# Routing stage: prefix counts of the expert choices as nine TensorE products instead of GpSimd sums, and x of the first batch as second load of its queue

## The chip, the cores and the metric

The kernel runs on one core of one Trainium2 chip. The metric is the device time of one execution in microseconds. The trace of one profiled execution gives every instruction with its engine, its source line and what it waited for; its times are counted from the start of the span, which is the stretch from the first to the last instruction.

## The reference

Eight batches of 512 tokens with 256 features pass through a gated cross attention (each query keeps its 32 best keys of 1024) and a mixture of eight experts, each as a residual. What matters here is the routing between the two. Every token chooses its two best experts. For the first choices and the second choices apart, a token's place with its expert is the number of tokens before it, over all batches, that made the same choice. A token whose place is 640 or more is dropped.

```python
top_k_probs, top_k_idx = jax.lax.top_k(router_probs, TOP_K)     # TOP_K = 2
for k in range(TOP_K):
    eid = top_k_idx[:, k]
    onehot = (eid[:, None] == experts[None, :]).astype(jnp.int32)
    pos_all = jnp.cumsum(onehot, axis=0) - 1
    pos = jnp.take_along_axis(pos_all, eid[:, None].astype(jnp.int32), axis=1)[:, 0]
    valid = pos < capacity                                      # 640
    ...
    disp = jnp.zeros((E, capacity, D), x_flat.dtype).at[eid, pos_c].add(jnp.where(valid[:, None], x_flat, 0.0))
```

## The kernel before

The program has five stages, one after the other: `project` (queries, keys and values), `attend`, `repair` (the few attention tiles that have to be done again), `route` and `experts`. A stage begins on all engines when the one before it has ended. The change lies in `route` alone, which stands between about 2209 and 2368 us of the span.

`route` works batch by batch, eight of them, each with four tiles of 128 tokens. For a batch TensorE turns the attention output by eight transposes (L1187), ScalarE copies the result to SBUF (L1257), TensorE multiplies by the output weights (L1198), and VectorE adds the bias and the residual (L1297, L1298) and normalises (L1301 to L1327). For the batch before it TensorE turns the normalised rows (L1211) and forms the router's logits (L1220), and VectorE takes the best two experts (`choose`, L1312 to L1321). Nothing but the order in each engine's own program and the semaphores sets the order of the work.

SyncE issues all plain loads and stores of the stage from one queue. First come wo (the output weights, 256 KB), gate (8 KB), bo (128 KB) and the scalars g_xattn and g_ffn; these five count on one semaphore, `w_in`. TensorE, ScalarE and VectorE begin only when all five have landed. Then come x of batch 0 and of batch 1 (512 KB each, L1137), and later a store and a load for every further batch.

The places are counted in four groups of two batches, that is of eight tiles. When the choices of a group are known, VectorE writes them as one-hot rows (`mark`, L1351): for each of 128 tokens and each tile 16 numbers, two choices by eight experts. GpSimd forms `sofar`, the running sum of these rows over the tiles before, one addition for each tile (L1167). TensorE then makes two products into the same PSUM region, `places`: the triangular matrix `upto` by the group's one-hot rows counts the tokens up to this one within its tile (L1238), and the matrix of ones by the group's `sofar` counts all tiles before it (L1240). Both have 128 columns, 8 tiles by 16. VectorE picks the count that belongs to each choice (L1363, L1365) and makes of it the row number to send to (`slots`, up to L1378). GpSimd sends the group's normalised rows there by sixteen indirect DMAs (L1171), and only then turns to the sums of the next group.

In TensorE's program the products of a group come after the logits of the group's last batch and before the transposes of the next batch; for the last group they are the last work of the stage. `experts` reads the rows that were sent.

Of the kernel before, what the change touches and what calls it, by code (L numbers as in the profile page):

```python
# [10 lines left out]
ALU = mybir.AluOpType  # L11
# [3 lines left out]
P = 128  # L15
# [1021 lines left out]
def route(nc, pl, io, scr, out, keep):  # L1037
# [10 lines left out]
    C = K2 * E  # L1048
    attn, x1 = keep["attn"], keep["x1"]
    DX = pl.DX  # L1050
    with ExitStack() as ctx:
# [30 lines left out]
        onehot = sb("r_onehot", [P, TT, K2, E])  # L1082
        sofar = sb("r_sofar", [P, TT + 1, K2, E])
        place = sb("r_place", [P, GT, K2, E])
# [30 lines left out]
        hot = sem("r_hot")  # L1115
        added = sem("r_added")
        counted = sem("r_counted")
# [7 lines left out]
        @block.sync  # L1125
        def _(sp):
            sp.dma_start(wo[:], io["woT"].rearrange("(k p) n -> p k n", p=P)).then_inc(w_in, 16)
            sp.dma_start(gate[:], io["gateT"].rearrange("(k p) n -> p k n", p=P)).then_inc(w_in, 16)
            sp.dma_start(bo[:], io["bo"].partition_broadcast(P)).then_inc(w_in, 16)
            for i, name in enumerate(("g_xattn", "g_ffn")):  # L1130
                sp.dma_start(g[:, i:i + 1], io[name][0].partition_broadcast(P)).then_inc(w_in, 16)

            def load(b, u, start):
                if not start:
                    sp.wait_ge(x1_done, QT * (b - 1))
                    keep_x1(b - 2)
                sp.dma_start(xin[:, u], io["x"][b].rearrange("(t p) d -> p t d", p=P)).then_inc(x_in[u], 16)  # L1137

            def keep_x1(b):
                sp.dma_start(out[b].rearrange("(t p) d -> p t d", p=P), x1[:, bass.ds(b * QT, QT), :]).then_inc(x1_kept, 16)  # L1140

            over(sp, B, 2, load)
            for b in (B - 2, B - 1):
                sp.wait_ge(x1_done, QT * (b + 1))
                keep_x1(b)
            sp.wait_ge(x1_kept, 16 * B)

        @block.gpsimd
        def _(pool):
# [11 lines left out]

            nc.gpsimd.memset(sofar[:, 0], 0.0).then_inc(added, 1)
            for g in range(NG):
                pool.wait_ge(hot, g + 1)
                for t in range(g * GT, (g + 1) * GT):
                    pool.wait_ge(added, t + 1)
                    nc.gpsimd.tensor_tensor(sofar[:, t + 1], sofar[:, t], onehot[:, t], ALU.add).then_inc(added, 1)  # L1167
                pool.wait_ge(slots_done, g + 1)
# [8 lines left out]
        def _(pe):  # L1177
# [53 lines left out]
            def places(g):  # L1231

                pe.wait_ge(hot, g + 1)
                pe.wait_ge(added, g * GT + GT)
                if g:
                    pe.wait_ge(picked, g)
                tiles = slice(g * GT, (g + 1) * GT)
                nc.tensor.matmul(ps_n[:, 0:GT * C], upto[:], onehot[:, tiles].rearrange("p t k e -> p (t k e)"),  # L1238
                                 start=True, stop=False)
                nc.tensor.matmul(ps_n[:, 0:GT * C], ones[:], sofar[:, tiles].rearrange("p t k e -> p (t k e)"),  # L1240
                                 start=False, stop=True).then_inc(counted, 1)

# [42 lines left out]
        def _(dve):  # L1285
            count = [0]

            def link(ins):
                count[0] += 1
                ins.then_inc(own, 1)  # L1290
                dve.wait_ge(own, count[0])
# [63 lines left out]
            def slots(g):  # L1355
# [4 lines left out]
                link(V.tensor_scalar(first[:, n, 1], first[:, n, 1], float(CAP), None, ALU.add))  # L1360
                dve.wait_ge(hot, g + 1)
                dve.wait_ge(counted, g + 1)
                V.tensor_tensor(flat(place[:]), ps_n[:, 0:GT * C], flat(onehot[:, n]), ALU.mult).then_inc(picked, 1)  # L1363
# [390 lines left out]
```

## Time and profile before

| what | us |
|---|---|
| median of 3 runs | 3109.03 (3107.15 to 3109.63) |
| the profiled execution | 3109.36 |
| its span | 3107.6 |
| TensorE busy (matmuls) | 2532.3, 81% of the span |
| VectorE busy | 2635.3, 85% |
| ScalarE busy | 1733.3, 56% |
| GpSimd busy | 1676.1, 54% |

The span is shorter than the execution's own time by what lies around the first and the last instruction. A share of busy time is a mean over five stages with different limits, so it says little of one stage. A row of the timeline has the start, the duration, the engine, the line, the operation with its tiles, the number of instructions merged in it, and in brackets how long the engine had been idle before and what released it. The granted clock of TensorE stands as a share of its full 2.4 GHz.

### The profile page before, as it was taken

How to read it: one execution, taken by the hardware profiler on the slowest of the kernel's cores; microseconds unless marked ns; L12 is line 12 of the kernel's file. 1: busy time of each engine (PE TensorE's matmuls, PEld its weight loads, DVE VectorE, ACT ScalarE, POOL GpSimd, SP SyncE). 2: the span in 40 equal slices, each digit the busy share in tenths (PEclk: the TensorE clock that was granted, in tenths of full speed). 3: DMA queues.
4: the chain of work that ended last, by engine and by line, in shares of the span. 5: the costliest groups of instructions: out<-in, count | busy, mean ns of one | idle time of the engine just before them, and what ended most of it. 6: DMA issues, size and time to landing. Idle time of an engine off the chain costs nothing. (4 is left out here: it accounts for less than half of the span.)

```text
span 3107.6 us, 67900 instructions
## 1 busy us (share of the span) xinstructions
PE 2532.3 (81%) x18774; PEld 1650.4 (53%) x18775; DVE 2635.3 (85%) x19297; ACT 1733.3 (56%) x2250; POOL 1676.1 (54%) x2652
## 2 busy tenths in 40 slices
PE   7846888888888888888888888863472999999998
PEld 4522444444444444444444444432362999999998
DVE  5748999999999999999999999967563777777774
ACT  2215888887878888888888788851120222222222
POOL 1006777778787878787878787840062111111121
PEclk9977999999999999999999999995675999999999
DMA  6962121211211211212112112102233222222221
GB/s 184 264 186 67 39 68 30 53 53 31 68 39 30 68 39 40 59 39 56 42 39 68 30 43 63 30 1 56 71 131 115 66 65 55 71 55 58 67 45 17
DMA packets 132583, 202.25 MB, mean 65 GB/s; under 512 B 24112, under 2 KB 99120, under 8 KB 129136
## 3 DMA queue, kind: packets, MB, share of 16 engines
q1 hardware_dynamic: 108048, 167.65, 20.0%
q0 software_dynamic: 17920, 29.52, 4.5%
q8 instruction: 149, 2.44, 0.3%
q14 instruction: 226, 1.85, 0.2%
q10 hardware_dynamic: 6240, 0.79, 0.2%
HBM read 130.48 MB, written 69.50 MB: 64 GB/s over the span
## 5 line engine op out<-in xcount | busy, mean ns | idle before, releaser
L596 DVE MAX8 a_cand<-a_sc 128x8 f32<-128x43 f32 (+1 forms) x12288 | 1602.6, 194 | 48.4 <-ACT a_sc L535 48.3
L702 POOL TENSOR_SCALAR a_side<-a_sc,a_top 128x1024 bf16<-128x1024 f32 x256 | 729.2, 2848 | 0.0
L535 ACT COPY a_sc<-a_ps_s 128x1024 f32<-128x1024 f32 x512 | 516.7, 1009 | 162.9 <-PE a_ps_s L437 155.9
L546 ACT ACTIVATE a_pT<-a_ps_e 128x1024 f32<-128x1024 f32 x512 | 521.8, 1019 | 86.1 <-PE a_ps_e L458 71.3
L454 PE MATMUL a_ps_e<-a_floor,a_onesb 128*128 128x256 bf16 x1024 | 283.8, 277 | 284.8 <-issue 145.8
L1461 POOL DMA_INDIRECT out<-e_y,e_xin x80 | 124.1, 1552 | 608.9 <-ACT e_y L1586 564.3
L722 POOL TENSOR_SCALAR a_gone<-a_cand,a_top 128x80 f32<-128x80 f32 x512 | 293.8, 574 | 261.0 <-DVE a_top L630 260.7
L456 PE MATMUL a_ps_e<-a_big,a_side 128*128 128x128 bf16 x4096 | 398.9, 220 | 0.0
L458 PE MATMUL a_ps_e<-a_qs,a_ks 99*128 99x512 bf16 x1024 | 395.0, 386 | 0.0
L528 ACT ACTIVATE a_side<-a_sc,a_next_under 128x1024 bf16<-128x1024 f32 x256 | 295.1, 1153 | 169.7 <-POOL a_next_under L715 169.7
L490 PE MATMUL a_ps_o<-a_pT,a_vs 128*32 128x512 f32 x2048 | 369.5, 603 | 1.1 <-ACT a_pT L546 1.1
L437 PE MATMUL a_ps_s<-a_ks,a_qs 96*128 96x512 bf16 x1024 | 319.1, 394 | 57.7 <-DMA a_vs<-scr_v 50.9
L1518 PE MATMUL e_ps_gu<-e_xh,e_wl 128*128 128x256 f32 x1280 | 361.9, 283 | 5.0 <-DVE e_xl L1597 5.0
L456 PEld LDWEIGHTS a_ps_e<-a_big,a_side 128*128 128x128 bf16 x4096 | 316.6, 98 | 92.2 <-issue 1.1
L1519 PE MATMUL e_ps_gu<-e_xl,e_wh 128*128 128x256 f32 x1280 | 361.5, 282 | 0.0
L1520 PE MATMUL e_ps_gu<-e_xh,e_wh 128*128 128x256 f32 x1280 | 361.3, 282 | 0.0
L454 PEld LDWEIGHTS a_ps_e<-a_floor,a_onesb 128*128 128x128 bf16 x1024 | 100.4, 98 | 490.5 <-ACT a_pT L546 260.5
L468 PE MATMUL a_ps_c<-a_side,a_row_of 128*16 128x512 bf16 x1024 | 314.0, 389 | 4.2 <-POOL a_side L702 2.8
L1578 ACT ACTIVATE e_th<-e_ps_gu 128x256 f32<-128x256 f32 x320 | 123.4, 386 | 323.0 <-PE e_ps_gu L1520 323.0
L1638 DVE SCALAR_TENSOR_TENSOR e_sg<-e_th,e_ps_gu 128x256 f32<-128x256 f32 x320 | 135.0, 422 | 184.0 <-ACT e_th L1578 168.9
L1518 PEld LDWEIGHTS e_ps_gu<-e_xh,e_wl 128*128 128x128 f32 x1280 | 242.3, 189 | 5.8 <-DVE e_xl L1597 5.8
L1519 PEld LDWEIGHTS e_ps_gu<-e_xl,e_wh 128*128 128x128 f32 x1280 | 242.4, 189 | 0.0
(211 smaller groups left out, 4908.0 us busy)
## 6 DMA issues: line engine op xcount, KB each, us to landing
scr_v<-p_vp SPq DMA_DIRECT2D x32, 512.0 KB, 5.9
a_vs<-scr_v SPq DMA_DIRECT2D x32, 512.0 KB, 5.9
a_mask<-in_mask SPq DMA_DIRECT2D x32, 512.0 KB, 6.8
scr_k<-p_kp SPq DMA_DIRECT2D x96, 128.0 KB, 2.4
a_ks<-scr_k SPq DMA_DIRECT2D x32, 384.0 KB, 4.7
a_qs<-scr_q SPq DMA_DIRECT2D x192, 64.0 KB, 5.2
scr_disp<-a_blank SPq DMA_DIRECT2D x16, 650.0 KB, 8.3
e_xin<-scr_disp SPq DMA_DIRECT2D x40, 260.0 KB, 2.7
```

What stands on the lines that cost most here:

```text
L437: mm = nc.tensor.matmul(ps_s[:, h * 512:(h + 1) * 512], qs[0:KR, u, j, qt * P:(qt + 1) * P], ks[0:KR, u, j, h * 512:(h + 1) * 512], start= ...
L454: nc.tensor.matmul(ps_e[:, i * S + HALF * P:(i + 1) * S], onesb[:], floor[:], start=True, stop=False)
L456: nc.tensor.matmul(ps_e[:, i * S + qt * P:i * S + (qt + 1) * P], side[:, (QT * H + qt) % SIDES, keys], big[:], start=False, stop=False)
L458: mm = nc.tensor.matmul(ps_e[:, i * S:(i + 1) * S], ks[:, u, j, keys], qs[:, u, j, :], start=False, stop=True)
L490: mm = nc.tensor.matmul(ps_o[VW * c:VW * (c + 1), :], vs[:, u, k, VW * j:VW * (j + 1)], pT[:, k, :], start=(half == 0), stop=(half == 1), ...
L535: nc.scalar.copy(sc[:, T % SCORES, :], ps_s[:]).then_inc(copied, 1)
L546: nc.scalar.activation(pT[:, 2 * n:2 * n + 2, :].rearrange("p k q -> p (k q)"), ps_e[:], ACT.Exp).then_inc(expd, 1)
L596: ins = nc.vector.max(c[:, 8 + n:8 + n + 7 * CH + 1:CH], sc[:, T % SCORES, pl.cut[n]:pl.cut[n + 1]])
L702: nc.gpsimd.tensor_scalar(side[:, T % SIDES, :], sc[:, T % SCORES, :], top[:, T // TILES % 2, T % TILES, pl.TOPK - 1:pl.TOPK], None, ALU.is_lt
L1518: nc.tensor.matmul(out, al, bh, start=(k == 0), stop=False)
L1519: nc.tensor.matmul(out, ah, bl, start=False, stop=False)
L1520: mm = nc.tensor.matmul(out, ah, bh, start=False, stop=(k == n - 1))
```

## The change

Two things are changed in `route`.

The running sums leave GpSimd. TensorE forms them with shifted products: the triangular matrix by the eight tiles of the group as before, then seven products of the matrix of ones by the first 7, 6, ... 1 tiles of the group, each added to the PSUM region 1, 2, ... 7 tiles further right, and a last product of ones by `sofar` of the group, the counts of all groups before it, read once for each of the eight tiles. `sofar` has now one entry for each group. VectorE keeps it: in `slots` it sums the group's one-hot rows over the tiles and adds the result to the group's entry. GpSimd only sends rows.

On SyncE's queue x of batch 0 comes directly behind wo, and bo comes before gate.

```diff
             sp.dma_start(wo[:], io["woT"].rearrange("(k p) n -> p k n", p=P)).then_inc(w_in, 16)
+            sp.dma_start(xin[:, 0], io["x"][0].rearrange("(t p) d -> p t d", p=P)).then_inc(x_in[0], 16)
+            sp.dma_start(bo[:], io["bo"].partition_broadcast(P)).then_inc(w_in, 16)
             sp.dma_start(gate[:], io["gateT"].rearrange("(k p) n -> p k n", p=P)).then_inc(w_in, 16)
-            sp.dma_start(bo[:], io["bo"].partition_broadcast(P)).then_inc(w_in, 16)
             ...
-                sp.dma_start(xin[:, u], io["x"][b].rearrange("(t p) d -> p t d", p=P)).then_inc(x_in[u], 16)
+                if b:
+                    sp.dma_start(xin[:, u], io["x"][b].rearrange("(t p) d -> p t d", p=P)).then_inc(x_in[u], 16)
             ...
-            nc.gpsimd.memset(sofar[:, 0], 0.0).then_inc(added, 1)
+            nc.gpsimd.memset(sofar[:, 0], 0.0).then_inc(summed, 1)
             for g in range(NG):
-                pool.wait_ge(hot, g + 1)
-                for t in range(g * GT, (g + 1) * GT):
-                    pool.wait_ge(added, t + 1)
-                    nc.gpsimd.tensor_tensor(sofar[:, t + 1], sofar[:, t], onehot[:, t], ALU.add).then_inc(added, 1)
                 pool.wait_ge(slots_done, g + 1)
             ...
                 pe.wait_ge(hot, g + 1)
-                pe.wait_ge(added, g * GT + GT)
+                pe.wait_ge(summed, g + 1)
                 if g:
                     pe.wait_ge(picked, g)
-                tiles = slice(g * GT, (g + 1) * GT)
-                nc.tensor.matmul(ps_n[:, 0:GT * C], upto[:], onehot[:, tiles].rearrange("p t k e -> p (t k e)"),
-                                 start=True, stop=False)
-                nc.tensor.matmul(ps_n[:, 0:GT * C], ones[:], sofar[:, tiles].rearrange("p t k e -> p (t k e)"),
-                                 start=False, stop=True).then_inc(counted, 1)
+                t0 = g * GT
+                wide = lambda n: onehot[:, t0:t0 + n].rearrange("p t k e -> p (t k e)")
+                nc.tensor.matmul(ps_n[:, 0:GT * C], upto[:], wide(GT), start=True, stop=False)
+                for d in range(1, GT):
+                    nc.tensor.matmul(ps_n[:, d * C:GT * C], ones[:], wide(GT - d), start=False, stop=False)
+                nc.tensor.matmul(ps_n[:, 0:GT * C].rearrange("p (t c) -> p t c", c=C), ones[:],
+                                 sofar[:, g].unsqueeze(1).broadcast_to([P, GT, C]), start=False, stop=True
+                                 ).then_inc(counted, 1)
             ...
                 dve.wait_ge(hot, g + 1)
+                if g + 1 < NG:
+                    link(V.tensor_reduce(here[:, g], onehot[:, n].rearrange("p t k e -> p (k e) t"), AX_X, ALU.add))
+                    dve.wait_ge(summed, g + 1)
+                    V.tensor_tensor(sofar[:, g + 1], sofar[:, g], here[:, g], ALU.add).then_inc(summed, 1)
                 dve.wait_ge(counted, g + 1)
```

## Rows read from the trace of the kernel before

**Rows 1.** The page: the chain that ended last, shares by line.

```profile
PE e_ps_gu L1518 5%; PE e_ps_gu L1519 5%; PE e_ps_gu L1520 5%; PE e_ps_y L1520 2%; PE e_ps_y L1518 2%; PE e_ps_y L1519 2%; PE e_ps_x L1510 1%; DVE e_wl L1621 0%; DMA e_raw<-in_wdT 0%; DMA e_raw<-in_wgT 0%; POOL out L1461 0%; DMA out<-e_y,e_xin 0%; DVE e_hl L1606 0%; DVE e_wh L1614 0%; DVE e_hh L1602 0%
```

**Rows 2.** Timeline of the stage's begin: start, duration, engine, line, idle before.

```profile
2211.63 0.43 SPq L1131 DMA_DIRECT2D r_g<-in_g_ffn  x1
2212.11 1.24 SPq L1137 DMA_DIRECT2D r_xin<-in_x  x2
...
2216.06 1.97 PE L1187 MATMUL r_ps_a<-r_ident,attn 128*128 128x128 f32 x8 [8.22 <-DMA r_g<-in_g_ffn]
...
2221.27 0.42 DVE L1297 TENSOR_TENSOR r_aO<-r_ps_w,r_bo 128x256 f32<-128x256 f32 x1 [12.08 <-PE r_ps_w L1198]
```

**Rows 3.** DMA issues of 2209 to 2212.2 us: count, KB, us to landing.

```profile
r_xin<-in_x SPq DMA_DIRECT2D x1, 512.0 KB, 5.5
...
r_g<-in_g_ffn SPq DMA_DIRECT2D x1, 0.5 KB, 4.4
```

**Rows 4.** Windows: length, busy by engine (count), PE clock, DMA share, GB/s.

```profile
2216.50:2217.00 0.50, 0.50 (x5) 0.50 (x4) 0.00 (x0) 0.00 (x0) 0.00 (x0) 0.50 1.09 385
```

**Rows 5.** Timeline around the first inner group.

```profile
2249.75 0.36 DVE L1351 TENSOR_TENSOR r_onehot<-r_lane,r_chosen 128x64 f32<-128x64 f32 x2
...
2250.20 2.41 POOL L1167 TENSOR_TENSOR r_sofar<-r_sofar,r_onehot 128x16 f32<-128x16 f32 x8 [39.10 <-DVE r_onehot L1351]
...
2252.46 0.77 PE L1238 MATMUL r_ps_n<-r_onehot,r_upto 128*128 128x128 f32 x2 [5.92 <-POOL r_sofar L1167]
...
2253.45 1.91 PE L1187 MATMUL r_ps_a<-r_ident,attn 128*128 128x128 f32 x8
2253.79 0.29 DVE L1363 TENSOR_TENSOR r_place<-r_ps_n,r_onehot 128x128 f32<-128x128 f32 x1 [1.85 <-PE r_ps_n L1240]
...
2258.68 0.42 DVE L1297 TENSOR_TENSOR r_aO<-r_ps_w,r_bo 128x256 f32<-128x256 f32 x1 [2.16 <-PE r_ps_w L1198]
```

**Rows 6.** Windows around the first inner group, columns as in rows 4.

```profile
2254.00:2256.00 2.00, 2.00 (x9) 1.69 (x8) 1.69 (x10) 1.17 (x2) 0.00 (x0) 0.50 0.00 0
...
2258.00:2260.00 2.00, 2.00 (x11) 1.77 (x10) 1.25 (x3) 0.00 (x0) 1.59 (x2) 0.99 0.19 67
```

**Rows 7.** Timeline of the second and third group: one-hot rows, next residual.

```profile
2278.35 0.36 DVE L1351 TENSOR_TENSOR r_onehot<-r_lane,r_chosen 128x64 f32<-128x64 f32 x2
...
2286.61 0.42 DVE L1297 TENSOR_TENSOR r_aO<-r_ps_w,r_bo 128x256 f32<-128x256 f32 x1 [1.54 <-PE r_ps_w L1198]
...
2306.08 0.36 DVE L1351 TENSOR_TENSOR r_onehot<-r_lane,r_chosen 128x64 f32<-128x64 f32 x2
...
2314.13 0.42 DVE L1297 TENSOR_TENSOR r_aO<-r_ps_w,r_bo 128x256 f32<-128x256 f32 x1 [1.34 <-PE r_ps_w L1198]
```

**Rows 8.** Weight loads of passes with 8 columns; loads and products of L437.

```profile
2316.92 1.86 PEld L1220 LDWEIGHTS r_ps_l<-r_gate,r_xT 128*128 128x128 f32 x16 [0.54 <-issue]
...
2325.30 3.49 PEld L1220 LDWEIGHTS r_ps_l<-r_gate,r_xT 128*128 128x128 f32 x16 [0.29 <-issue]
...
L437 PEld LDWEIGHTS a_ps_s<-a_ks,a_qs x1024: 95/98/181, 245.5 to 2048.4; 96*128 96x128 bf16 x171
L437 PE MATMUL a_ps_s<-a_ks,a_qs x1024: 377/382/634, 245.5 to 2048.6; 96*128 96x512 bf16 x171
```

**Rows 9.** Timeline of the last group and the stage's end.

```profile
2330.82 0.36 DVE L1351 TENSOR_TENSOR r_onehot<-r_lane,r_chosen 128x64 f32<-128x64 f32 x2
...
2333.82 2.33 POOL L1167 TENSOR_TENSOR r_sofar<-r_sofar,r_onehot 128x16 f32<-128x16 f32 x8
...
2337.29 0.29 DVE L1363 TENSOR_TENSOR r_place<-r_ps_n,r_onehot 128x128 f32<-128x128 f32 x1 [5.82 <-PE r_ps_n L1240]
...
2340.80 0.99 POOL L1171 DMA_INDIRECT scr_disp<-r_xn,r_slot_to  x1 [4.64 <-DVE r_slot_to L1378]
...
2359.99 0.97 POOL L1171 DMA_INDIRECT scr_disp<-r_xn,r_slot_to  x1 [0.31 <-issue]
2368.21 0.38 SPq L1477 DMA_DIRECT2D e_raw<-in_wgT  x1
```

More of the change, by code:

```diff
@@ L1082, in route @@
         onehot = sb("r_onehot", [P, TT, K2, E])
-        sofar = sb("r_sofar", [P, TT + 1, K2, E])
+        here = sb("r_here", [P, NG, C])
+        sofar = sb("r_sofar", [P, NG, C])
         place = sb("r_place", [P, GT, K2, E])
@@ L1115, in route @@
         hot = sem("r_hot")
-        added = sem("r_added")
+        summed = sem("r_summed")
         counted = sem("r_counted")
```

## The prediction

> **What bounds the kernel now.** I first read the chain of work that ended last: it is nearly all TensorE in the expert stage, and no line of the routing stage stands in it [rows 1]. That chain starts over at every stage boundary: the expert stage's first transfer is issued at 2368.21, after the last row of the routing stage has been sent [rows 9]. So the routing stage, 2209 to 2368 us of the span, has an end of its own, and what is taken out of its own chain moves everything behind it as a block. I then read that stage as a timeline. The reader is to see three things. It begins with a wait for small loads [rows 2]. In the middle VectorE and TensorE hand over to each other, with GpSimd between them once for each group of two batches [rows 5]. It ends with sixteen sends by GpSimd that nothing covers [rows 9].
>
> **The loads (x of the first batch second).** Before, the scalar g_ffn is issued at 2211.63, and its landing, 4.4 us later, starts TensorE at 2216.06 [rows 2, 3]. TensorE, ScalarE and VectorE all wait for the same count of five loads, wo, gate, bo and the two scalars. x was issued at 2212.11 and landed 5.5 us later, at 2217.6 [rows 2, 3]. VectorE needs it first at 2221.27, and what it waited for there was TensorE's product [rows 2]. Landing x earlier is therefore worth nothing: it was 3.7 us early already. Its cost is that gate, bo and the scalars are issued one issue later on SyncE's queue. Two x issues took 1.24 us, so 0.62 us each [rows 2]. If g_ffn keeps its 4.4 us, TensorE starts 0.6 us later. The bounds are these. Below: g_ffn now lands as its twin g_xattn might, which was issued one place before it and had no x directly behind it; I give that -0.4 us at most, an estimate, since g_ffn's 4.4 us is the only row for it. Above: the whole of x passes first, 512 KB at the 385 GB/s that the queue moved while x came in [rows 4], 1.4 us. I take +0.6 us, and it counts in full, because every engine of the stage hangs on that start.
> The Trainium skill, page DMA: Bandwidth & Descriptors, section Queues, rings and completion order, says that on each DMA engine descriptors are consumed in ring order. This speaks against the move, as bytes of x put ahead of the scalars are then waited for: by that rule the price is nearer the upper bound than the 0.6.
>
> **The three inner groups (after batches 1, 3 and 5).** In the first of them the one-hot rows are done at 2249.75 + 0.36 = 2250.11. GpSimd takes them up 0.09 us later and adds tile by tile for 2.41 us. TensorE starts its two products at 2252.46, goes on to the transposes of the next batch at 2253.45 (so 0.99 us for two products), and VectorE takes the counts 0.34 us later, at 2253.79 [rows 5]. The change takes GpSimd's sums out and puts seven products in: nine instead of two. A product of this type is two passes, as x2 on the row of one product shows [rows 5]. A pass with 128 x 128 weights costs its weight load even when only 8 columns stream: sixteen such passes took 3.49 us in the last batch, 0.218 each, and 1.86 us, 0.116 each, one batch before [rows 8]. That is the clock at 1.2 and at 2.4 GHz. Nor does the shared matrix of ones save its loads: where two products share weights in the attention stage, there are 1024 loads for 1024 products [rows 8]. Around the first group the granted clock was 0.50, that is 1.2 GHz [rows 6]. So 14 more passes cost 14 x 0.218 = 3.05 us there. TensorE can start at 2250.11 + 0.09 = 2250.20, ends at 2250.20 + 0.99 + 3.05 = 2254.24, and the transposes behind it in its queue start 0.79 us later than before. VectorE's counts are as late. By this alone the next batch's residual, which waited 2.16 us for TensorE [rows 5], is 0.79 us later in each group.
> Against that stands the clock. It was back at 2.4 GHz from 2258 on [rows 6], 5.5 us after the products had begun at 2252.46 [rows 5]. The products now begin 2.26 us earlier. If the rise comes as long after their start, it falls at 2250.11 + 5.6. The eight passes of the transposes end at 4.13 + 8 x 0.218 = 5.9 us after the one-hots, and the eight passes of the first half of the output product behind them run at 2.4 GHz: 256 columns each, at most 2 x 0.116, so 1.9 us in all (an estimate). VectorE would start the residual at about 7.8 us after the one-hots. Before it was 8.57 us (2258.68 - 2250.11), and 7.90 and 7.69 us in the second and third group [rows 5, 7]. That gives -0.8, -0.1 and +0.1. The bounds for a group are +0.79 (no earlier rise) and, with everything at 2.4 GHz, the wait of the residual as it stood, -2.16, -1.54 and -1.34 [rows 5, 7]. The three together give -0.8 and lie between -5.0 and +2.4; as the bounds reach further down than up, I take -1.0 us.
> VectorE's two new instructions (a sum over tiles and one addition) read no more than the 128 x 128 that the row of the count takes 0.29 us for, so 0.6 us at most, and lie in the 1.85 us that it waited for TensorE [rows 5]. Were that wait gone, they would cost 0.6 us a group. The running count that they write is needed by TensorE one group later, 28 us on. GpSimd's own work shrinks, and its sends start when the slots are done, as before.
>
> **The last group.** Here GpSimd's sums were late. The one-hots are done at 2330.82 + 0.36 = 2331.18, but GpSimd is still sending the third group's rows and starts adding at 2333.82. VectorE gets the counts at 2337.29, the first send is at 2340.80, the last at 2359.99, and the next stage at 2368.21 [rows 9]. After the change TensorE needs only the one-hots and an old count: 2331.18 + 0.09 + 0.99 + 3.05 + 0.34 = 2335.65, so 1.64 us earlier. GpSimd ended the old sends before 2333.82, so it is not late for the new ones. The sixteen sends stay as they are and move as a block. At 2.4 GHz the 18 passes would take 18 x 0.116 = 2.1 us, and the gain would be some 3.6 us. TensorE had been at 1.2 GHz shortly before [rows 8], so I take -2.0, nearer to that end.
> The Trainium skill, page TensorE: Matmul & The Clock Gate, section Back-to-back issue gap, gives the isolated spacing of products by the columns streamed. The seven products stream 448 columns where seven full ones would stream 896, so by that rule the added passes cost half, 1.5 us instead of 3.05. The row of the 8-column passes speaks against it [rows 8], and the page itself adds that weight loads share in the spacing.
>
> **Sum.** +0.6 - 1.0 - 2.0 = -2.4 us. The profiled execution took 3109.36 us, of which the span is 3107.6; it would take 3107.0. The median of the runs shown, 3109.03, lies 0.3 lower, so I forecast 3106.6 us.
>
> **The rivals.**
> (a) TensorE becomes the bound in the inner groups: the nine products run at 1.2 GHz, the rise comes when it came, and each of the three groups is 0.79 us later. 2.4 + 0.6 - 1.64 = +1.4 us, 3110.4, slower than before. It decides as soon as the three delays and the later start exceed the last group's gain. For it: clock 0.50 around the products [rows 6]. Against it: the earlier start of TensorE's work.
> (b) A narrow product costs its columns: four groups at 1.5 us less, of which the inner three can use only their waits. About -2.4 - 4 = -6.4 us, or 3102.6. The 8-column row is against it [rows 8]. It is the rule of the Trainium skill's page TensorE: Matmul & The Clock Gate named above.
> (c) x holds the scalars back for its whole transfer: +1.4 in place of +0.6, 3107.4. The order of the queue is for it; the share of idle time in the queue before x is not shown at that place.
> (d) The clock is at 2.4 GHz in all four groups: up to -5.0 - 3.6 + 0.6 = -8 us, 3101.0.
> (e) It does not matter: GpSimd's sends bind the last group anyway. The 3.5 us between the counts and the first send, with GpSimd idle [rows 9], speak against this; 3109.
>
> **How the numbers follow.** Forecast 0.58, (a) 0.13, (b) 0.05, (c) 0.14, (d) 0.04, (e) 0.06. The forecast's own range is some 2.5 us to either side, from the unknown rise of the clock and the run to run spread of 2.5 us that the three times show. Leaving out (b), (d) and part of (a), the range is 3103.0 to 3110.0. 0.2% is 6.2 us, about what a measurement can tell from no change: faster needs 3102.8 or less, which takes (d), half of (b) and a tail of the forecast, 0.07; slower needs 3115.2, which no case reaches, 0.01; within it 0.92.
>
> **What would show it.** TensorE's first product of the stage should start 0.4 us early to 1.4 us late, by when g_ffn lands. Each group should show 18 passes that start 0.1 us after the one-hots, at 0.22 us each. The wait of VectorE for the counts should be longer in the inner groups and shorter, by about 1.6 us, in the last; the first send of the last group should come 4.5 + 3.5 = 8.0 us after the one-hots instead of 9.6. The forecast is wrong if passes of few columns cost less than 0.2 us at 1.2 GHz, if the stretch from the stage's start to the last one-hots moves by more than 3 us, or if the expert stage behind it changes its length.

## The result

The changed kernel takes 3114.7 us (median; 3111.6 to 3118.3), the kernel before 3109.9 us beside it. The ratio is 1.0015, 95% interval 1.0009 to 1.0021: slower by 4.8 us, 2.8 to 6.5 by the interval. The forecast was 3106.6 us, 3103.0 to 3110.0. The profiled execution took 3114.59 us with a span of 3112.3; against 3109.36 before it is 5.2 us longer.

Between the two traces these 5.2 us lie as follows. The stages before `route` ended 0.9 us earlier, `route` took 1.3 us more (159.8 against 158.5, from the issue of wo to the issue of the first expert weights), `experts` 4.3 us more (743.7 against 739.4), and 0.5 us lies around the span. So most of the loss stands in a stage that the change does not touch.

**The loads after.** The rows are the issue of the last scalar, its size and us to landing from the view of DMA issues, and TensorE's first work:

```profile
2211.25 0.43 SPq L1133 DMA_DIRECT2D r_g<-in_g_ffn  x1
...
r_g<-in_g_ffn SPq DMA_DIRECT2D x1, 0.5 KB, 4.0
...
2215.32 0.90 PE L1186 MATMUL r_ps_a<-r_ident,attn 128*128 128x128 f32 x3 [8.41 <-DMA r_g<-in_g_ffn]
```

wo is issued at 2208.75, so TensorE starts 6.57 us after it; before it was 6.38 (2209.68 to 2216.06).

**The first group after** (rows of the timeline: start, duration, engine, line, operation, in brackets the wait and its releaser). The lines are moved by the change: L1354 is the one-hot rows, L1239 to L1242 the nine products, L1186 and L1197 the next transposes and output product, L1300 the residual.

```profile
2249.13 0.36 DVE L1354 TENSOR_TENSOR r_onehot<-r_lane,r_chosen 128x64 f32<-128x64 f32 x2
2249.55 0.80 PE L1239 MATMUL r_ps_n<-r_onehot,r_upto 128*128 128x128 f32 x2 [3.49 <-DVE r_onehot L1354]
2250.14 3.01 PE L1241 MATMUL r_ps_n<-r_onehot,r_ones 128*128 128x112 f32 x14
2252.98 0.77 PE L1242 MATMUL r_ps_n<-r_sofar,r_ones 128*128 128x128 f32 x2
2253.55 1.92 PE L1186 MATMUL r_ps_a<-r_ident,attn 128*128 128x128 f32 x8
2253.80 0.29 DVE L1370 TENSOR_TENSOR r_place<-r_ps_n,r_onehot 128x128 f32<-128x128 f32 x1 [1.90 <-PE r_ps_n L1242]
...
2258.58 0.42 DVE L1300 TENSOR_TENSOR r_aO<-r_ps_w,r_bo 128x256 f32<-128x256 f32 x1 [2.06 <-PE r_ps_w L1197]
```

The products start 0.06 us after the one-hot rows' end, the seven new ones take 3.01 us, which is 0.215 us a pass, and the counts come 4.67 us after the one-hots' start instead of 4.04 [rows 5]. All that was foreseen. What was not is the clock. The windows of TensorE over the first and the third group after (columns: stretch, length, busy time of TensorE's products PE, its weight loads PEld, VectorE DVE, ScalarE ACT and GpSimd POOL with counts, granted clock, busy share of the DMA engines, GB/s):

```profile
2252.00:2254.00 2.00, 2.00 (x11) 2.00 (x11) 0.20 (x1) 0.00 (x0) 0.00 (x0) 0.50 0.00 0
...
2256.00:2258.00 2.00, 2.00 (x7) 1.61 (x6) 0.49 (x4) 0.09 (x1) 0.27 (x1) 0.56 0.06 16
2258.00:2260.00 2.00, 2.00 (x11) 1.73 (x10) 1.33 (x3) 0.00 (x0) 1.70 (x2) 1.00 0.19 67
...
2312.00:2314.00 2.00, 2.00 (x6) 1.64 (x6) 1.10 (x7) 0.58 (x1) 0.00 (x0) 0.50 0.00 0
2314.00:2316.00 2.00, 2.00 (x7) 1.61 (x6) 0.11 (x1) 0.00 (x0) 1.68 (x2) 0.56 0.18 67
```

In a window that begins at 0.50, ends at 1.00 and has a mean of 0.56, the clock rose 0.24 us before the end, here at 2257.76 and 2315.76. The products of these groups had begun at 2249.55 and 2306.27, so the clock came 8.2 and 9.5 us after them. In the kernel before it came 5.6 us after them in the first group; in the third the window of before gives 2312.64, 3.9 us after the start at 2308.74:

```profile
2312.00:2314.00 2.00, 2.00 (x9) 1.71 (x8) 0.72 (x5) 0.26 (x1) 0.43 (x1) 0.84 0.00 0
```

**The last group and the stage's end after:**

```profile
2332.58 0.36 DVE L1354 TENSOR_TENSOR r_onehot<-r_lane,r_chosen 128x64 f32<-128x64 f32 x2
...
2337.35 0.29 DVE L1370 TENSOR_TENSOR r_place<-r_ps_n,r_onehot 128x128 f32<-128x128 f32 x1 [4.11 <-PE r_ps_n L1242]
...
2340.86 0.97 POOL L1170 DMA_INDIRECT scr_disp<-r_xn,r_slot_to  x1 [6.56 <-DVE r_slot_to L1385]
...
2360.01 0.97 POOL L1170 DMA_INDIRECT scr_disp<-r_xn,r_slot_to  x1 [0.30 <-issue]
...
2368.57 0.38 SPq L1484 DMA_DIRECT2D e_raw<-in_wgT  x1
```

The counts come 4.77 us after the one-hots' start, before 6.47 [rows 9], a gain of 1.70 us. But the one-hots themselves come later: 83.45 us after those of the first group, where it was 81.07 [rows 5, 9].

**The expert stage.** Two places differ. The first is its first weight load: the DMA issues of the first 7 us, after and then before (KB, us to landing), with the instruction queue's line where there is one:

```profile
q14 instruction: 1, 0.01, 0.3%
...
e_raw<-in_wgT SPq DMA_DIRECT2D x1, 1024.0 KB, 5.7
```
```profile
e_raw<-in_wgT SPq DMA_DIRECT2D x1, 1024.0 KB, 4.9
```

VectorE waits for this load and TensorE's first transposes wait for VectorE. They start 19.0 us into the stage instead of 17.7. The second place is the one at which VectorE's loop over experts (`Fori`, experts 3 and 4, then 5 and 6) jumps back, some 460 us into the stage. VectorE's first row behind the jump, before and after:

```profile
2826.87 0.69 DVE L1597 TENSOR_TENSOR e_xl<-e_ps_x,e_xh 128x512 fp32r<-128x512 f32 x1 [2.83 <-issue]
```
```profile
2830.22 0.69 DVE L1604 TENSOR_TENSOR e_xl<-e_ps_x,e_xh 128x512 fp32r<-128x512 f32 x1 [3.73 <-issue]
```

"issue" says that VectorE waited for nothing that the profile shows. In the 4.5 us ahead of these rows the DMA view has one instruction packet on queue q14 before and two after:

```profile
q14 instruction: 1, 0.01, 0.5%
```
```profile
q14 instruction: 2, 0.02, 1.4%
```

Behind this pause TensorE's clock fell in the changed kernel, from 1.00 to 0.66 in the mean of five microseconds, with 29 products instead of some 44:

```profile
2831.00:2836.00 5.00, 5.00 (x29) 5.00 (x30) 0.85 (x2) 0.76 (x2) 2.89 (x2) 0.66 0.46 52
2836.00:2841.00 5.00, 5.00 (x44) 5.00 (x43) 4.56 (x15) 1.16 (x4) 0.00 (x0) 1.00 0.22 53
```

### The profile page after: what moved, and what is told of

Read it like the earlier page. It is cut to its first block and busy times, and to the rows that moved or that the text cites. A ratio compares the mean times of both kernels' runs of the same rounds, so it can differ in the third digit from the quotient of the medians.

```text
span 3112.3 us, 67985 instructions
## 1 busy us (share of the span) xinstructions
PE 2544.3 (82%) x18830; PEld 1664.3 (53%) x18831; DVE 2637.1 (85%) x19303; ACT 1731.8 (56%) x2250; POOL 1668.0 (54%) x2620
## 5 line engine op out<-in xcount | busy, mean ns | idle before, releaser
L596 DVE MAX8 a_cand<-a_sc 128x8 f32<-128x43 f32 (+1 forms) x12288 | 1637.5, 206 | 48.2 <-ACT a_sc L535 48.2
L437 PE MATMUL a_ps_s<-a_ks,a_qs 96*128 96x512 bf16 x1024 | 318.3, 393 | 57.5 <-DMA a_vs<-scr_v 50.8
```

The lines of the kernel that those rows point to most:

```text
L437: mm = nc.tensor.matmul(ps_s[:, h * 512:(h + 1) * 512], qs[0:KR, u, j, qt * P:(qt + 1) * P], ks[0:KR, u, j, h * 512:(h + 1) * 512], start= ...
L596: ins = nc.vector.max(c[:, 8 + n:8 + n + 7 * CH + 1:CH], sc[:, T % SCORES, pl.cut[n]:pl.cut[n + 1]])
```

## The experiments

The table has what the runs' traces and times say, each stretch from one trace. "Intervals" are from the one-hots of one group to those of the next. "Counts" is from the last group's one-hots' start to VectorE's first use of the counts. "Landing" and "pause" are the two places of the expert stage named above. A median with an interval of the ratio was timed beside the kernel before; one without is a single time.

| kernel | intervals, sum | counts | `route` | landing | pause | `experts` | time, ratio |
|---|---|---|---|---|---|---|---|
| before | 28.6 + 27.7 + 24.7 = 81.1 | 6.5 | 158.5 | 4.9 | 2.83 | 739.4 | 3109.9 |
| changed | 28.9 + 27.8 + 26.7 = 83.5 | 4.8 | 159.8 | 5.7 | 3.73 | 743.7 | 3114.7, 1.0015 [1.0009, 1.0021] |
| e1 before again | 25.1 + 31.4 + 24.9 = 81.4 | 6.5 | 159.5 | 5.0 | 2.83 | 739.7 | 3111.3 |
| e2 loads only | 28.5 + 27.5 + 24.9 = 80.9 | 6.5 | 158.1 | 4.8 | 2.97 | 739.5 | 3109.6, 0.9999 [0.9990, 1.0008] |
| e3 counts only | 29.0 + 27.8 + 26.7 = 83.6 | 4.8 | 160.4 | 5.6 | 3.82 | 744.1 | 3114.7, 1.0015 [1.0006, 1.0024] |
| e4 VectorE's part only | 27.4 + 28.8 + 24.9 = 81.0 | 6.5 | 158.8 | 5.6 | 3.89 | 741.0 | 3112.5, 1.0008 [0.9999, 1.0017] |
| e5 last group only | 27.4 + 28.9 + 24.9 = 81.2 | 4.8 | 157.9 | 5.1 | 2.90 | 740.4 | 3108.3, 0.9995 [0.9986, 1.0004] |
| e6 changed, 119 more | 29.0 + 27.8 + 26.8 = 83.5 | 4.8 | 160.1 | 5.0 | 2.88 | 739.4 | 3111.1, 1.0003 [0.9994, 1.0012] |
| e7 before, 128 more | 28.6 + 27.5 + 24.9 = 81.0 | 6.5 | 158.8 | 4.9 | 2.88 | 739.6 | 3111.1 |
| e9 full width (e8, a single run) | 26.6 + 25.4 + 24.6 = 76.7 (76.3) | 4.3 (4.3) | 152.2 (151.4) | 5.6 (5.5) | 3.94 (3.73) | 741.1 (740.7) | 3104.6, 0.9984 [0.9975, 0.9993] (3102.4) |
| e10 full width, 119 more | 26.6 + 25.4 + 24.7 = 76.7 | 4.3 | 152.6 | 5.0 | 2.84 | 739.5 | 3101.7, 0.9976 [0.9967, 0.9985] |
| e11 before, extra products | 26.4 + 29.8 + 24.2 = 80.4 | 7.3 | 158.1 | 4.9 | 2.95 | 739.7 | 3109.3, 1.0001 [0.9991, 1.0010] |
| e12 before, 40 more | 27.4 + 28.9 + 25.2 = 81.5 | 6.0 | 158.9 | 5.0 | 2.88 | 739.6 | 3110.3 |

**Which part loses.** Three runs take the change apart, beside one of the kernel before as it is. e2 has only the new order of the loads, e3 only the counts.

> The kernel before, unchanged: a second look at its stages. Every theory expects the median of before within its spread of some 3 us. What is asked is how far the three places vary by themselves that were longer in the changed kernel: the first weight load of the expert stage (4.9 us before, 5.7 after), the pause of VectorE in the middle of that stage (2.8 us before, 3.7 after) and TensorE's clock behind it. If they are a matter of VectorE's program, they come out as before: 2.8 us and no fall of the clock. If they are chance, they may come out either way.

> Only the loads are reordered, the counts are formed as before. Theory loads (the 512 KB of x hold the scalars back): +0.6 to +1.4 us. Theory program (VectorE's longer program costs the time, in the expert stage): no change, within 0.5 us, as VectorE's program is the one of before. Theory counts: no change.

> Only the counts move to TensorE, the loads stay in the old order. Theory loads: -2 to -3 us, since the loss would be in the order of the loads. Theory program: +4 to +5 us, as in the whole change, with a VectorE pause of 3.7 us in the expert stage. Theory counts (the nine products delay the inner groups): +1 to +2 us, all of it inside the routing stage.

e2 stands at 0.9999 and e3 at 1.0015: the loads cost nothing that can be measured, and the counts are the whole loss. In both e2 and the changed kernel the stage's first work after the loads starts 6.5 to 6.6 us after the issue of wo; the eight kernels with the old order (before, e1, e3, e4, e5, e7, e11, e12) have 5.8 to 6.8, so no difference shows there either.

**VectorE's part alone.** The kernel before, with the same number of VectorE instructions added at the same place as in the change, their results unused; TensorE and GpSimd do what they did.

```diff
+                if g + 1 < NG:
+                    link(V.tensor_reduce(spare[:, g], onehot[:, n].rearrange("p t k e -> p (k e) t"), AX_X, ALU.add))
+                    dve.wait_ge(own, count[0])
+                    V.tensor_tensor(spare_sum[:, g], spare[:, g], spare[:, g], ALU.add).then_inc(spared, 1)
                 dve.wait_ge(counted, g + 1)
```

> The kernel before with VectorE's six new instructions alone (three sums over tiles and three additions, into tiles that nothing reads), so that VectorE's program is as long as in the changed kernel; GpSimd forms the sums and TensorE makes two products, as before. Theory program: +3 to +4.5 us, the pause of VectorE in the middle of the expert stage 3.7 instead of 2.8 us and the clock of TensorE down to 1.2 GHz behind it. Theory counts and theory loads: no change, within 0.5 us, as the six instructions lie in VectorE's wait for the counts.

`route` is as before (158.8), so the instructions themselves cost nothing there. But the landing and the pause are those of the changed kernel, and `experts` is 741.0 instead of 739.4. The fall of the clock behind the pause, which the text expected, did not come. The time, 1.0008 with an interval from 0.9999 to 1.0017, agrees with those 1.6 us but would not show them by itself. So these two places follow VectorE's program, not TensorE's or GpSimd's. Is it the length, or where the code of the loop comes to lie? With the waits among them the change adds nine instructions to VectorE's program.

```diff
             slots(NG - 1)
+            for i in range(119):
+                V.memset(spare[:, i:i + 1], 0.0)
```

e6 puts these 119 into the changed kernel, e7 puts 128 and e12 puts 40 into the kernel before. VectorE has nothing to do there until the next stage; the 119 took 2.89 us of that time.

> The changed kernel, with 119 very small VectorE instructions (a memset of one column each) behind its last work of the routing stage, where VectorE waits some 25 us for the last sends. With the change's nine added VectorE instructions these make 128. In the trace an instruction packet of VectorE's size is 8192 bytes; I take it as 128 instructions. Theory A (what counts is where the code of the expert stage lies in such blocks): VectorE's pause in the middle of the expert stage is 2.8 us again instead of 3.7, the first weights land 4.9 us after their issue instead of 5.7, TensorE's first transposes start 17.5 to 18 us into the stage, and TensorE's clock no longer falls behind the pause; the expert stage takes 739.5 to 741 us and the time is 3 to 4 us below the changed kernel, so 1 to 2 us above the kernel before, which is what the routing stage lost. Rival B (what counts is the length of VectorE's program): pause 3.7 to 3.9 us, expert stage 743.7 or more, time as the changed kernel's. Rival C (the expert stage is longer for TensorE's 28 added rows or for GpSimd's shorter program): as B, but with the pause at 2.8.

> The kernel before with 128 of the same small VectorE instructions at the same place. Theory A (place in blocks): everything in the expert stage as in the kernel before: pause 2.8 us, first weights 4.9 us. Rival B (length): pause 3.7 us or more, first weights 5.6 us, expert stage 741 us.

> The kernel before with 40 of the small VectorE instructions behind its last work of the routing stage, for a second place of the expert stage's code in its blocks. Nine more gave a pause of 3.7 to 3.9 us and first weights after 5.6 to 5.7 us, 128 more 2.88 and 4.9. Theory A (it matters whether a block's border falls in front of the loop's start): pause again of one of the two sizes, 2.8 to 3.0 or 3.7 to 3.9, and the first weights 4.9 to 5.1 or 5.6 to 5.7 independently of it. Rival B (the pause grows with the place): something between or beyond, such as 4.5 us.

With 119 more the pause is short again:

```profile
2829.54 0.69 DVE L1607 TENSOR_TENSOR e_xl<-e_ps_x,e_xh 128x512 fp32r<-128x512 f32 x1 [2.88 <-issue]
```
```profile
q8 instruction: 1, 0.02, 1.4%
q14 instruction: 1, 0.01, 0.6%
```

One packet on q14 instead of two (the one on q8 did not lengthen the pause), the first weights after 5.0 us, `experts` 739.4, no fall of the clock, and the ratio 1.0003 instead of 1.0015, although VectorE's program is longer still. That is theory A: it is the place that counts, not the length. What is left, +2.1 us by the medians and +1.0 by the ratio (interval -1.9 to +3.7), agrees with the 1.6 us that `route` is longer. Of the places tried, 0, 40 and 128 instructions further give the short pause and the early landing; 9 gives the long ones, in each of the five kernels that had it (changed, e3, e4, e8, e9). In the changed kernel and e3 the clock fell behind the long pause, in e4, e8 and e9 it did not. What decides that was not tried. With the fall `experts` took 743.7 and 744.1, without it 740.7 to 741.1, so some 2.9 us go with it. (Both kernels also have an earlier fall, 39 us into the stage. e1, e2, e5 and e12 have one too, at 37 to 39 us, and take 739.5 to 740.4, so it explains little of this.)

**The last group alone.** GpSimd sums the inner groups as before; TensorE forms the counts of the last group with the nine products.

```diff
-                pe.wait_ge(added, g * GT + GT)
+                pe.wait_ge(added, g * GT + (GT if g + 1 < NG else 1))
...
+                if g + 1 < NG:
+                    nc.tensor.matmul(ps_n[:, 0:GT * C], ones[:], sofar[:, tiles].rearrange("p t k e -> p (t k e)"),
+                                     start=False, stop=True).then_inc(counted, 1)
+                    return
...
+                for d in range(1, GT):
+                    nc.tensor.matmul(ps_n[:, d * C:GT * C], ones[:], wide(GT - d), start=False, stop=False)
...
```

> The kernel before, with one thing of the change: only in the last group do TensorE's nine products form the counts; the three inner groups stay with GpSimd's sums, the loads stay in the old order, VectorE's program is unchanged. Theory A (the loss has two places: the inner groups, where TensorE's products take 0.65 us more each and the clock rises no earlier, and the expert stage, where VectorE's nine added instructions move its code): here neither is touched, so the last group's counts come 1.5 to 1.7 us earlier, the stretch from the stage's start to the choices of the last group stays at 121 us, the routing stage is 156.5 to 157 us long instead of 158.5, the expert stage stays at 739.4 to 739.8, and the time is 1.5 to 2 us below the kernel before. Rival B (any change of the routing stage's length costs the expert stage some us by its phase): the routing stage gets shorter and the expert stage is 741 to 744 all the same. Rival C (the products of the last group are of no use because GpSimd's old sends hold it): routing stage 158.5, time as before.

The last group's counts come 4.76 us after its one-hots, 1.7 us earlier, as expected, and VectorE's program, landing and pause are as before or nearly (5.1, 2.90). `route` was 157.9, 0.6 us shorter and not 1.5 to 2; `experts` was 740.4. What hides the gain lies ahead of the change: from the issue of wo to the first group's one-hots e5 took 41.0 us, the kernel before 40.1, and over all runs this stretch goes from 39.7 to 41.0. The time is 0.8 us lower in the median, and the interval reaches from -4.4 to +1.2 us: the gain of the last group is there in the trace but is not shown in the time.

**The width of the passes.** The changed kernel, but all seven products stream 128 columns. Each group's one-hot rows stand behind eight tiles of zeros, and the product for a shift of d tiles reads from d tiles further back.

```diff
-        onehot = sb("r_onehot", [P, TT, K2, E])
+        onehot = sb("r_onehot", [P, NG, 2 * GT, K2, E])
...
+            nc.gpsimd.memset(onehot[:, :, 0:GT], 0.0).then_inc(made, 1)
...
-                    nc.tensor.matmul(ps_n[:, d * C:GT * C], ones[:], wide(GT - d), start=False, stop=False)
+                    nc.tensor.matmul(ps_n[:, 0:GT * C], ones[:], back(d), start=False, stop=False)
```

> The changed kernel, but every one of the seven products streams the full 128 columns: the one-hot rows of each group stand behind eight tiles of zeros, and the product for a shift of d tiles reads from d tiles further back. Same count of passes, of waits and of VectorE instructions. Theory A (the pass costs its weight load, and TensorE's clock rises late in the changed kernel because narrow passes keep the engine less busy): a pass costs 0.22 to 0.25 us at 1.2 GHz as the narrow ones did (0.215 to 0.218), and the clock rises some 5 us after the products' start, as before, instead of 6.5 to 9.5 us; the choices of the last group come 1 to 3 us earlier than in the changed kernel (117.1 us after TensorE's start of the stage). Rival B (the rise does not depend on the width): rises 6.5 to 9.5 us after the products' start, choices at 117 us or later.

> The changed kernel with the seven products at full width, as in the run of one look (3102.4 us), now timed. There the routing stage was 151.3 us long (158.5 before, 159.9 changed) and the granted clock rose 4.3, 5.3 and 3.2 us after the products' start (8.2, 6.5 and 9.5 changed). Theory A (the width of the passes, through the clock, decides): median 3102 to 3106, the routing stage 151 to 155 us, the expert stage 740.8 to 741.5 as VectorE's code still lies nine instructions further. Rival B (the one look was a chance of the clock's timing): median 3109 to 3113, routing stage 157 us or more.

(In the third group of e8, the rise came 3.8 us after the products' start, not the 3.2 that the second of these texts says.) Timed, the kernel takes 3104.6 us, 0.9984 of the kernel before, and `route` 152.2 us. This is theory A: the pass costs the same and the clock comes earlier. Its size was not foreseen: the three intervals are 7 us shorter than in the changed kernel, where the first text has 1 to 3. Nor do the rows show its reason, a less busy engine: over the passes TensorE is busy 2.00 of 2.00 us with either width (2252 to 2254 above, 2254 to 2256 in e10). e10 has in addition the 119 instructions.

> Both repairs: the seven products at full width, and 119 small VectorE instructions behind its last work of the routing stage, so that its code for the expert stage lies 128 instructions further instead of nine. Theory A (two independent causes): routing stage 151 to 155 us, pause 2.8 to 2.9, first weights 5.0 us, expert stage 739.4 to 740; median 1 to 2 us below the full-width kernel without them, 3101 to 3104.5, and 5 to 8 us below the kernel before. Rival B (the effects are not additive): as the full-width kernel.

e10 takes 3101.7 us, ratio 0.9976 (0.9967 to 0.9985): some 7.5 us faster than the kernel before and the best version of the study. In the traces the two repairs add up (`route` 152.6, `experts` 739.5); by the times alone the intervals of e9 and e10 overlap. Its first and third group (the lines moved by one or two more):

```profile
2252.57 0.80 PE L1240 MATMUL r_ps_n<-r_onehot,r_upto 128*128 128x128 f32 x2 [3.48 <-DVE r_onehot L1355]
2253.16 3.19 PE L1242 MATMUL r_ps_n<-r_onehot,r_ones 128*128 128x128 f32 x14
...
2260.36 0.42 DVE L1301 TENSOR_TENSOR r_aO<-r_ps_w,r_bo 128x256 f32<-128x256 f32 x1 [0.83 <-PE r_ps_w L1199]
...
2304.63 0.80 PE L1240 MATMUL r_ps_n<-r_onehot,r_upto 128*128 128x128 f32 x2 [3.96 <-DVE r_onehot L1355]
...
2312.01 0.42 DVE L1301 TENSOR_TENSOR r_aO<-r_ps_w,r_bo 128x256 f32<-128x256 f32 x1 [0.45 <-PE r_ps_w L1199]
```
```profile
2257.00:2259.00 2.00, 1.76 (x10) 1.47 (x10) 1.70 (x9) 1.07 (x2) 0.00 (x0) 0.90 0.00 0
...
2308.00:2310.00 2.00, 1.76 (x13) 1.52 (x12) 1.03 (x5) 0.73 (x2) 0.00 (x0) 0.85 0.08 27
```

The fourteen passes stream 1792 columns and not 896. Their row is 0.18 us longer than the narrow ones', by the last pass, but their weight loads take 3.11 us in both kernels (changed first, then e10), and the counts come 4.66 us after the one-hots' start (changed kernel 4.67):

```profile
2249.93 3.11 PEld L1241 LDWEIGHTS r_ps_n<-r_onehot,r_ones 128*128 128x128 f32 x14
```
```profile
2252.95 3.11 PEld L1242 LDWEIGHTS r_ps_n<-r_onehot,r_ones 128*128 128x128 f32 x14
```

The means of 0.90 and 0.85 put the rise at 2257.4 and 2308.6, 4.8 and 4.0 us after the products' start. In the changed kernel it was 8.2 and 9.5. VectorE's residual waits 0.83 us, where it waited 2.06 in the changed kernel.

Is the earlier rise only a matter of when the clock had fallen? In the first group that is excluded. The windows ahead of it, of the changed kernel and of e10, begin at 1.00 and end at 0.50, so their means put the fall at 2247.5 and 2250.6, in both kernels 2.0 us before the products' start:

```profile
2247.00:2249.00 2.00, 0.00 (x0) 0.00 (x0) 1.83 (x20) 1.49 (x2) 0.00 (x0) 0.63 0.55 184
```
```profile
2250.00:2252.00 2.00, 0.00 (x0) 0.00 (x0) 1.83 (x21) 1.49 (x2) 0.00 (x0) 0.65 0.55 181
```

The earlier rise is not the whole gain, though. In e10 the clock also stayed up longer. In the second group the residual comes 7.9 us after the one-hots' end, as in the kernel before, and still the interval is 2.3 us shorter. The gain lies in the group's second batch, where TensorE had 1.00 in e10 and 0.50 in the changed kernel (which comes first here) and in the kernel before:

```profile
2294.00:2298.00 4.00, 4.00 (x11) 3.12 (x10) 2.49 (x9) 0.00 (x0) 3.09 (x4) 0.50 0.93 292
```
```profile
2294.00:2298.00 4.00, 4.00 (x22) 3.54 (x23) 3.79 (x14) 0.26 (x1) 3.09 (x4) 1.00 1.00 306
```

**Is it the clock alone?** e11 leaves the counts with GpSimd and adds seven full-width products, their results unused, in the place where TensorE waits for GpSimd.

```diff
                 pe.wait_ge(hot, g + 1)
...
+                for d in range(1, GT):
+                    nc.tensor.matmul(ps_n[:, GT * C:2 * GT * C], ones[:], onehot[:, tiles].rearrange("p t k e -> p (t k e)"),
+                                     start=d == 1, stop=d == GT - 1)
                 pe.wait_ge(added, g * GT + GT)
```

> The kernel before, its counts still by GpSimd's sums, with seven added full-width products of ones by the group's one-hot rows into unused columns of the same PSUM tile, in the place where TensorE waits for GpSimd (the results are not used). Theory A (what the full-width kernel gained in the inner groups is TensorE's clock, and no matter of who forms the counts): the products start 0.1 us after the one-hots, the two real ones follow some 0.7 us later than before, but the clock rises 3 to 5.5 us after the first product instead of coming 5.5, 4.4 and 3.9 us after the later start of the kernel before (2252.46, 2281.01, 2308.74), so that in the three groups together the choices of the last group come 3 to 6 us earlier than the 114.6 us of before; the last group keeps its 6.7 us; routing stage 153 to 156 us, expert stage 739.4 to 739.8, median 3104 to 3107. Rival B (the gain comes from taking GpSimd's sums away): no gain, each group 0.7 us later, routing stage 160.5 us, 3111.

Neither came out: 3109.3 us, ratio 1.0001, `route` 158.1. The first interval shrank as theory A says (28.6 to 26.4), and the second gave it back (27.7 to 29.8). The timeline of the second group shows how:

```profile
2277.98 0.36 DVE L1354 TENSOR_TENSOR r_onehot<-r_lane,r_chosen 128x64 f32<-128x64 f32 x2
...
2279.53 0.97 POOL L1171 DMA_INDIRECT scr_disp<-r_xn,r_slot_to  x1 [0.30 <-issue]
2280.52 2.33 POOL L1167 TENSOR_TENSOR r_sofar<-r_sofar,r_onehot 128x16 f32<-128x16 f32 x8
...
2282.60 0.80 PE L1241 MATMUL r_ps_n<-r_onehot,r_upto 128*128 128x128 f32 x2 [0.85 <-POOL r_sofar L1167]
```

The one-hots are there at 2278.34, but GpSimd is still sending the first group's rows and begins to add at 2280.52. TensorE has finished the extra products and waits for it, and the clock rises 8.9 us after the one-hots, where it was 6.6 in the kernel before. The same stands in e1, where nothing was changed: the first interval was 25.1, with the clock rising 2.9 us after the products' start, and in the second, 31.4 long, GpSimd began to add 3.1 us after the one-hots. In the seven kernels whose inner groups GpSimd sums without extra products (before, e1, e2, e4, e5, e7, e12) the sum of the three intervals is 80.9 to 81.5, however the single ones fall. In e1 and e11 the sends take back what a group gained; in e4, e5 and e12 they hold the second group's sums by only 0.5 us, and the clock rises later there (8.2 us after the one-hots). So in these runs neither half gained alone: e11 had the early clock and kept the sums on GpSimd, the change took them off and had the late clock. e11 also pays for its extra products, 0.8 us in the last group's counts.

## Why the prediction was wrong

**The loads.** Foreseen +0.6 us. g_ffn was issued 0.55 us later behind wo, as foreseen, but landed after 4.0 us instead of 4.4, so the trace shows +0.2 at the stage's start; that is within what kernels with the old order differ by, and e2's time shows no difference. x's bytes did not hold the scalars back by a whole transfer: rival (c) is out by the trace; e2's interval, 3 us to either side, could not tell.

**The inner groups.** Foreseen -1.0, measured +2.4 (81.07 to 83.45). The prices of the products were right: 0.215 us a pass against 0.218, and 0.6 to 0.7 us later counts in each group against 0.79. The step that failed is the sentence "If the rise comes as long after their start". It took the product's start for what brings the clock and put the rise 5.6 us after the one-hots. After their end it came 8.3, 6.6 and 9.6 us in the changed kernel, and 7.9, 6.6 and 6.2 us before. So the third group lost 2.0 us, the first 0.3 and the second 0.1, where the forecast had +0.1, -0.8 and -0.1. The form of these passes, which I used for their price only, decided the clock: with 128 columns in each, the rise came 4.9, 5.6 and 4.0 us after the one-hots (e10), near what I had assumed. There the rest of the step held: at a rise after 5.6 us the residual came after 7.9, forecast 7.8, and the three residuals together came 1.0 us earlier than in the kernel before, the forecast's -1.0. The groups gained 4.4 us; the other 3.4 us lie behind the residuals, where the clock stayed up longer, which the prediction did not consider. Rival (a), "TensorE becomes the bound in the inner groups", comes nearest to what happened in `route`. That its bound for the three groups, +2.4, is the measured sum is luck: it is made of three times 0.79, and the trace has 0.3, 0.1 and 2.0.

**The last group.** Foreseen -2.0, with -1.64 at 1.2 GHz; measured -1.70. The passes were at 1.2 GHz and the step was right but for the 0.4 us added for the chance of 2.4 GHz. The first send came 7.9 us after the one-hots' end, forecast 8.0, so rival (e), that GpSimd's old sends bind it, is out.

**Narrow passes.** Rival (b), a product costs its columns, is out: with 896 columns and with 1792 the fourteen weight loads take 3.11 us, and the counts come 4.67 and 4.66 us after the one-hots' start. The price of a pass follows its weight load, as the 8-column rows said [rows 8].

**VectorE's instructions.** The prediction gave them 0.6 us in a wait of 1.85, and that held: `route` did not grow in e4. What it lacked is the second price of an instruction, the place of all the code behind it. It closed with "the expert stage behind it changes its length" as a way to be wrong, put the term at nothing in its sum and had no rival for it. This is the second step that failed, and by size the first: that stage made 4.3 of the 5.2 us, 1.6 to 1.7 from the landing and the pause (e4, e9 against e10), the rest where the clock fell behind the pause.

The sum by the traces: +0.2 for the loads, +0.1 up to the first one-hots, +2.4 for the inner groups, -1.7 for the last one and +0.3 between the last send and the next stage (8.22 before, 8.56 after, cause open) are the +1.3 of `route`; with +4.3 for `experts`, -0.9 before `route` and 0.5 around the span they make 5.2.

## What to carry to other kernels

Before extra TensorE work is put down at a price per pass, look at the granted clock of that place and ask whether the new work will bring the rise earlier or later; here passes of the same price made 6.8 us of difference by their width alone (83.5 against 76.7 us). An engine that is filled in every round, as GpSimd is here by its sends, can take back what another gains, so relieve it and speed the other up together. Before a single stretch of one trace is put down to a change, take the unchanged kernel a second time: here one interval moved from 28.6 to 25.1 us by itself, while the sum of three stayed within half a microsecond. Where an engine has a loop that jumps back, compare the pause at the jump before and after any change of the code ahead of it: it can move by a microsecond though no line of that stage was touched, and a few instructions in an idle place can set it right.

## What the hardware showed that I had not expected

- **Code position.** Nine added VectorE instructions made the pause at a backward jump 3.7 to 3.9 us instead of 2.8 to 3.0 and the landing of a 1 MB load 5.5 to 5.7 us instead of 4.8 to 5.1; 40 and 128 did not. In the pause the DMA view has two instruction packets on q14 instead of one, and one falls into that load. That these packets are what makes the two places longer is read from their coming together in every run; no run moves the packets alone. The Trainium skill, page Runtime: NRT & Kernel Launch, section Instruction fetch mechanics, says that a taken branch whose target is outside the fetched blocks has to fetch it before execution goes on. The traces agree: 2.83 us with one packet, 3.73 with two.
- **Clock.** TensorE was busy 2.00 of 2.00 us in windows during and behind the narrow products and still at 0.50. With full-width products the granted clock was back at 2.4 GHz 4.0 to 5.5 us after their start (e9, e10), with narrow ones after 6.6 to 9.5 us (changed kernel, e6), in the three groups of each.
- **Passes.** At 1.2 GHz fourteen passes with 128 x 128 weights loaded them in 3.11 us, with 16 to 112 columns in a pass and with 128 in each alike.
